# The handwritten orders of work of four engines, renewed from self-attention to the first products of the shared network

## The chip, the core and the metric

The kernel runs on one core of a Trainium2 chip. The metric is the device time of one launch in microseconds (us); lower is better. Engines are named as in the profile: PE multiplies matrices, PEld loads its weights, DVE (VectorE), ACT (ScalarE) and POOL (GpSimd) work on elements, SP issues most DMAs.

## What is computed

One decoder layer in fp32 for 8 batches of 112 tokens with 512 features (896 tokens): self-attention with latent queries and keys, cross-attention to a context, and a shared network with 16 routed experts, with a layer norm after each.

```python
x = layernorm(x + attn(x))      # 16 heads; q = [q_nope, rope(q_pe)], k = [k_nope, rope(k_rope)]; causal softmax
x = layernorm(x + xattn(x, ctx))  # 16 heads of 32; keys and values from ctx @ Wkv_expand.T; causal softmax
x = layernorm(x + shared(x) + routed(x))  # two shared gelu networks, top 2 of 16 experts
```

## The kernel before

Every product is split in three: `x = hi + lo`, and hi*hi, hi*lo and lo*hi are summed in PSUM. So a product's result is copied out of PSUM twice, by ACT (the hi part) and then by DVE (the lo part), before its bank is free.

**Self-attention** goes over 4 groups of 4 heads (`NG`, `GH`). Its steps are items of lists, one list for each engine, each item a kind and a number. Kinds: `A` (joined weights), `E` and `O` (rope products), `Q` (queries), `G` (scores, masked by DVE into `sT`), `S` (PE turns the scores, DVE takes the row maximum, ACT the four exponentials), `N` (DVE inverts the row sums, POOL multiplies them in), `T` (PE turns the probabilities, ACT and DVE split them), `B` (output weights joined with values), `Z` (probabilities times latents, split by ACT and DVE), `W` (the product of the group's output, added to `acc` by DVE), `SA` and `SB` (splitting weights that a DMA brought to `stage`), `R` (splitting the turned queries; SP then packs them with 16 DMAs for each half, line 557). `NEXT` marks an item of the following group. `turns` writes out a `..._PRE` list, the body in a loop of three passes (`ATT_PE` and so on), and a `..._LAST` list.

**Cross-attention** goes over 4 groups in the same way with `X_PRE`, `X_..` (three passes) and `X_LAST`. `K`, `Q`, `V` are keys, queries and values; `K` goes from DVE to SP, which spreads it with four DMAs (line 589) to `kb`, and PE waits for these before `S`. `Z` is copied by ACT and DVE to `zf`, and POOL splits it (lines 650 and 653) for `W`. `L`, `LK`, `X` split weights. In the last lists `STAT`, `VAR`, `ROOT`, `ROW` are steps of the layer norm, `U1` and `U2` turn its result, `F` (POOL) splits the first weights of the shared network, `FF` are its first products; `K` and `CX` in `ATT_LAST` begin cross-attention.

What orders the engines: each works through its own list and waits on semaphores inside an item. Products of the kinds A, E, O, Q, G, B, W, K and V take PSUM banks 6 and 7 in turn by their place in PE's list, and each waits until the one two places before has left its bank (`bank_free`). `S` waits for the exponentials of the score tile two before it, `T` for POOL's product, `Z` for the split of `T`.

The change touches the lists, the tile `warm` and `function_ready`, which calls a function once so that ACT loads its table early. After `X_LAST` the kernel runs 8 stages of the shared network with the expert blocks between them; the change leaves them as they are.

## Time and profile before

| | us |
|---|---|
| median of 3 runs (838.66 to 839.76) | 839.01 |
| the profiled execution | 837.5 |
| its span | 835.7 |
| PE busy | 816.4 (98%) |
| DVE busy | 530.9 (64%) |
| ACT busy | 456.7 (55%) |
| POOL busy | 241.1 (29%) |

The profile is of one execution. PE's matmuls are pipelined: one begins before the one before it has ended, so PE's lost time is read from the distances of starts. The loop of self-attention runs from 68.5 to 274.2 us (three passes), its last list to 322.8, cross-attention's loop from 338.6 to 423.7 (three passes), its last list to 458.

### The profile page before, as it was taken

The page shows a single profiled execution, that of the slowest core. Times are in us where ns is not written, and L with a number is a line of the kernel's source. Part 1 is how long each engine was busy: PE and PEld are TensorE (multiplying, and loading weights), DVE is VectorE, ACT ScalarE, POOL GpSimd, SP SyncE. Part 2 cuts the span into 40 slices and gives each one's busy share as a digit, 9 for nine tenths or more (in the row PEclk, how much of TensorE's full clock was granted, in tenths as well). Part 3 has the DMA queues.
Part 4 walks back from the last instruction along what each step waited for, and adds up shares of the span by engine and source line. Part 5 has one row for each costly group of instructions (what it writes and reads, how often), then busy time and mean ns, then how long its engine had stood idle before and what let it go on. Part 6 is the DMA issues. An engine that isn't in the chain of part 4 may idle for free.

```text
span 835.7 us, 13323 instructions
## 1 busy us (share of the span) xinstructions
PE 816.4 (98%) x4270; PEld 698.3 (84%) x4270; DVE 530.9 (64%) x994; ACT 456.7 (55%) x1189; POOL 241.1 (29%) x284
## 2 busy tenths in 40 slices
PE   7999999999999999999999999999999999999997
PEld 5887888888888888888867788888889888888885
DVE  4657746854854777778797566355655656656466
ACT  6427445643743666887786524254746737557050
POOL 0142311231132141655562005312332332320520
PEclk9999999999999999999999999999999999999999
DMA  9113413241260343312220306444555645634522
GB/s 347 66 45 114 179 56 85 92 168 41 72 230 17 83 163 93 88 41 58 56 74 1 101 3 226 150 125 140 190 181 173 227 140 176 211 131 139 141 73 89
DMA packets 42749, 99.99 MB, mean 120 GB/s; under 512 B 16016, under 2 KB 24080, under 8 KB 41584
## 3 DMA queue, kind: packets, MB, share of 16 engines
q1 hardware_dynamic: 31648, 61.62, 23.1%
q0 software_dynamic: 11056, 37.79, 13.9%
q8 instruction: 27, 0.44, 0.2%
q14 instruction: 18, 0.15, 0.1%
HBM read 71.59 MB, written 20.97 MB: 111 GB/s over the span
## 4 chain that ended last, share of the span: by engine, by line
PE 89%; DVE 4%; ACT 3%; issue 1%; DMA 1%; SPq 1%; DVEq 0%; ACTq 0%
PE ps L1553 71%; PE ps L1716 4%; PE ps L1900 2%; PE ps L1574 2%; PE ps L1613 2%; PE ps L1890 2%; PE ps L1724 1%; PE ps L1784 1%; ACT Pt L890 1%; DMA kb<-kx 1%; PE ps L1902 1%; SPq L589 1%; DVE stats L1173 1%; PE ps L1568 1%; PE ps L1605 0%
## 5 line engine op out<-in xcount | busy, mean ns | idle before, releaser
L645 POOL TENSOR_TENSOR Pt<-Pt,rowinv 112x448 f32<-112x448 f32 x64 | 59.6, 936 | 169.2 <-DVE rowinv L1157 169.0
L890 ACT ACTIVATE Pt<-ps,negmax 112x112 f32<-112x112 f32 x256 | 87.2, 358 | 26.9 <-DVE negmax L1150 26.4
L1553 PE MATMUL ps<-x2T_hi,ws_hi 128*128 128x448 f32 x256 | 95.3, 372 | 1.6 <-DVE x2T_lo L1094 1.6
L1553 PE MATMUL ps<-x2T_hi,ws_lo 128*128 128x448 f32 x256 | 93.6, 366 | 0.0
L1553 PE MATMUL ps<-x2T_lo,ws_hi 128*128 128x448 f32 x256 | 93.6, 365 | 0.0
L1553 PE MATMUL ps<-w_hi,h_hi 128*128 128x512 f32 x224 | 89.9, 401 | 0.0
L1021 ACT ACTIVATE hf<-ps,b 128x448 f32<-128x448 f32 x64 | 40.6, 634 | 88.0 <-PE ps L1553 87.3
L1553 PE MATMUL ps<-w_hi,h_lo 128*128 128x512 f32 x224 | 88.5, 395 | 0.0
L1553 PE MATMUL ps<-w_lo,h_hi 128*128 128x512 f32 x224 | 88.4, 395 | 0.0
L1094 DVE TENSOR_TENSOR h_lo<-hf,h_hi 128x448 fp32r<-128x448 f32 x64 | 39.9, 623 | 45.8 <-ACT h_hi L1022 45.6
L1439 DVE TENSOR_TENSOR acc<-ps,acc 128x512 f32<-128x512 f32 x56 | 38.6, 689 | 45.0 <-PE ps L1553 45.0
L769 POOL DMA_INDIRECT wg<-in_wtab,ix_i x29 | 31.0, 1069 | 112.0 <-DVE ix_i L1424 61.2
L1553 PE MATMUL ps<-qkT_hi,wa_hi 128*128 128x448 f32 x144 | 54.2, 377 | 1.3 <-DVE wa_lo L1097 0.6
L819 ACT ACTIVATE PT_hi<-ps 112x448 fp32r<-112x448 f32 x64 | 34.8, 545 | 37.2 <-PE ps L1613 37.1
L1167 DVE TENSOR_TENSOR acc<-ps,acc 128x512 f32<-128x512 f32 x56 | 38.6, 689 | 25.8 <-PE ps L1553 25.7
L890 ACT ACTIVATION_READ_ACCUMULATOR Pt<-ps,negmax 112x1 f32 x256 | 53.7, 210 | 0.0
L1553 PEld LDWEIGHTS ps<-x2T_hi,ws_hi 128*128 128x128 f32 x256 | 48.1, 188 | 6.4 <-POOL ws_lo L653 2.0
L1553 PE MATMUL ps<-qkT_hi,wa_lo 128*128 128x448 f32 x144 | 52.6, 366 | 0.0
L1553 PE MATMUL ps<-qkT_lo,wa_hi 128*128 128x448 f32 x144 | 52.6, 365 | 0.0
L1553 PEld LDWEIGHTS ps<-x2T_lo,ws_hi 128*128 128x128 f32 x256 | 48.2, 188 | 4.3
L1553 PEld LDWEIGHTS ps<-x2T_hi,ws_lo 128*128 128x128 f32 x256 | 48.1, 188 | 4.1
L1553 PEld LDWEIGHTS ps<-w_hi,h_lo 128*128 128x128 f32 x224 | 42.1, 188 | 10.1
(289 smaller groups left out, 2212.3 us busy)
## 6 DMA issues: line engine op xcount, KB each, us to landing
stage<-in_wf SPq DMA_DIRECT2D x30, 513.0 KB, 4.2
rows_in<-in_zeros SPq DMA_DIRECT2D x30, 256.0 KB, 5.5
xs<-rows_in POOLq DMA_DIRECT2D x29, 256.0 KB, 4.3
rows_out<-yb POOLq DMA_DIRECT2D x29, 256.0 KB, 2.7
stage<-in_wb SPq DMA_DIRECT2D x4, 1280.0 KB, 5.7
stage<-in_wa SPq DMA_DIRECT2D x8, 512.0 KB, 4.4
qr<-ro_hi SPq DMA_DIRECT2D x64, 56.0 KB, 1.9
qr<-ro_lo SPq DMA_DIRECT2D x64, 56.0 KB, 1.9
```

What stands on the lines that cost most here:

```text
L645: nc.gpsimd.tensor_tensor(p, p, rowinv[0:S, b % 2, :].unsqueeze(2).broadcast_to([S, GH, S]), ALU.mult).then_inc(norm_done, 1)
L769: return pool.indirect_dma_start(dst, None, table, bass.IndirectOffsetOnAxis(ap=index, axis=0))
L819: return nc.scalar.activation(dst, src, ACT.Copy, **kw)
L890: last = nc.scalar.activation(Pt[0:S, b % 2, h * S:(h + 1) * S], ps[0:S, b % 2, h * S:(h + 1) * S], ACT.Exp, bias=negmax[0:S, b % 2, h:h + 1],
L1021: nc.scalar.activation(hf[:, q % 4, :], ps[:, q % 3, 0:HALF], ACT.Gelu, bias=bias)
L1094: return nc.vector.tensor_tensor(dst, src, f32(hi), ALU.subtract)
L1167: nc.vector.tensor_tensor(acc[:, t, :], ps[:, 6 + at.bank, :], acc[:, t, :], ALU.add)\
L1439: V.tensor_tensor(acc2[:, t, :], ps[:, 3 + m % 2, :], (acc2 if n else acc)[:, t, :], ALU.add)\
L1553: ins = mm(dst, w, x, start=start and i == 0, stop=stop and i == len(ops) - 1, skip_group_check=not (start and stop))
L1574: ins = mm(ps[0:S, b, :], w, x, start=k == 0 and i == 0, stop=k == KD - 1 and i == 2, skip_group_check=True)
L1613: ins = nc.tensor.transpose(ps[0:S, 2 + b % 2, h * S:(h + 1) * S], Pt[0:S, b % 2, h * S:(h + 1) * S], ident[0:S, 0:S])
L1716: ins = mm(heads(bank[0:S, 0:GH * S]), w, x, start=i == 0, stop=i == len(ops) - 1)
```

## The change

The lists of PE, ACT, DVE and POOL are written in another order from the body of self-attention's loop to the last list of cross-attention; their items are the same (`SB`, `SA` and `R` do nothing on PE). `ATT_PRE` is unchanged. `warm` gets a second column, so that the call for Sqrt and the one for Exp write different elements. The core of the diff, with the lists of which the prediction speaks:

```diff
 ATT_PE = [
-    ("SB", 1), ("S", 0), ("G", 1), ("Q", 2, 1), ("G", 2), ("S", 1), ("B", 0), ("SB", 2), ("B", 1), ("T", 0), ("S", 2),
-    ("Q", 3, 1), ("B", 2), ("Z", 0), ("T", 1), ("G", 3), ("G", 4), ("Z", 1), (NEXT, "SA", 0), ("S", 3), ("S", 4),
-    ("T", 2), ("G", 5), (NEXT, "O", 0), ("B", 3), ("Z", 2), (NEXT, "SA", 1), ("S", 5), (NEXT, "E", 0), ("T", 3),
-    ("G", 6), ("W", 0), (NEXT, "A", 0), ("G", 7), (NEXT, "SA", 2), ("T", 4), (NEXT, "R", 0), ("Z", 3), ("W", 1),
-    (NEXT, "E", 1), (NEXT, "A", 1), ("S", 6), ("T", 5), ("Z", 4), ("S", 7), ("W", 2), (NEXT, "A", 2), ("Z", 5),
-    (NEXT, "O", 1), (NEXT, "R", 1), ("W", 3), ("T", 6), (NEXT, "Q", 0, 0), (NEXT, "Q", 1, 0), ("T", 7),
-    (NEXT, "Q", 2, 0), ("Z", 6), (NEXT, "SB", 0), ("W", 4), (NEXT, "Q", 3, 0), ("Z", 7), (NEXT, "Q", 0, 1), ("W", 5),
-    (NEXT, "G", 0), (NEXT, "Q", 1, 1), ("W", 6)]
+    ("S", 0), ("G", 1), ("Q", 2, 1), ("G", 2), ("S", 1), ("B", 0), ("B", 1), ("SB", 1), ("S", 2), ("T", 0),
+    (NEXT, "SA", 0), ("Q", 3, 1), ("B", 2), ("Z", 0), ("T", 1), ("G", 3), ("G", 4), ("B", 3), ("Z", 1), ("S", 3),
+    ("T", 2), ("S", 4), ("G", 5), (NEXT, "O", 0), ("G", 6), (NEXT, "SA", 1), ("T", 3), ("Z", 2), (NEXT, "E", 0),
+    ("S", 5), ("W", 0), ("G", 7), ("SB", 2), (NEXT, "R", 0), ("S", 6), ("Z", 3), (NEXT, "A", 0), ("T", 4), ("S", 7),
+    (NEXT, "E", 1), ("W", 1), (NEXT, "R", 1), (NEXT, "A", 1), (NEXT, "SB", 0), ("Z", 4), ("T", 5), ("W", 2),
+    (NEXT, "A", 2), (NEXT, "O", 1), ("W", 3), (NEXT, "Q", 0, 0), ("Z", 5), (NEXT, "Q", 1, 0), ("T", 6),
+    (NEXT, "Q", 2, 0), (NEXT, "Q", 3, 0), ("W", 4), ("T", 7), ("Z", 6), (NEXT, "G", 0), ("Z", 7), (NEXT, "Q", 0, 1),
+    ("W", 5), (NEXT, "SA", 2), (NEXT, "Q", 1, 1), ("W", 6)]
...
 ATT_ACT = [
     ("SB", 1), ("S", 0), ("Q", 2, 1), ("SB", 2), ("B", 0), ("B", 1), ("T", 0), ("S", 1), ("Q", 3, 1), ("B", 2),
-    ("Z", 0), ("T", 1), ("S", 2), (NEXT, "SA", 0), (NEXT, "SA", 1), ("T", 2), ("S", 3), ("Z", 1), ("B", 3), ("Z", 2),
-    ("T", 3), (NEXT, "SA", 2), (NEXT, "E", 0), ("S", 4), (NEXT, "A", 0), ("T", 4), ("Z", 3), (NEXT, "O", 0), ("S", 5),
-    (NEXT, "R", 0), ("T", 5), (NEXT, "A", 1), ("S", 6), ("Z", 4), (NEXT, "E", 1), (NEXT, "A", 2), ("Z", 5),
-    (NEXT, "O", 1), ("S", 7), (NEXT, "SB", 0), (NEXT, "Q", 0, 0), ("T", 6), (NEXT, "Q", 1, 0), (NEXT, "Q", 2, 0),
-    ("Z", 6), ("T", 7), (NEXT, "Q", 3, 0), (NEXT, "R", 1), ("Z", 7), (NEXT, "Q", 0, 1), (NEXT, "Q", 1, 1)]
+    ("T", 1), ("S", 2), (NEXT, "SA", 0), ("B", 3), ("Z", 0), ("T", 2), ("Z", 1), ("S", 3), (NEXT, "SA", 1),
+    (NEXT, "SA", 2), ("T", 3), ("Z", 2), ("S", 4), ("S", 5), (NEXT, "R", 0), (NEXT, "A", 0), ("Z", 3), ("T", 4),
+    (NEXT, "O", 0), (NEXT, "A", 1), ("Z", 4), (NEXT, "O", 1), ("T", 5), ("S", 6), (NEXT, "E", 0), (NEXT, "A", 2),
+    (NEXT, "Q", 0, 0), (NEXT, "E", 1), ("S", 7), ("Z", 5), (NEXT, "Q", 1, 0), ("T", 6), (NEXT, "Q", 2, 0),
+    (NEXT, "Q", 3, 0), (NEXT, "SB", 0), ("T", 7), ("Z", 6), ("Z", 7), (NEXT, "R", 1), (NEXT, "Q", 0, 1),
+    (NEXT, "Q", 1, 1)]
...
 ATT_DVE = [
-    ("S", 0), ("SB", 1), ("G", 1), ("N", 0), ("Q", 2, 1), ("G", 2), ("SB", 2), ("B", 0), ("S", 1), ("B", 1), ("T", 0),
-    ("N", 1), ("S", 2), ("Q", 3, 1), ("B", 2), ("T", 1), ("Z", 0), ("G", 3), ("N", 2), ("G", 4), ("S", 3),
-    (NEXT, "SA", 0), ("G", 5), ("T", 2), ("N", 3), ("Z", 1), (NEXT, "O", 0), ("S", 4), ("B", 3), (NEXT, "SA", 1),
-    (NEXT, "E", 0), ("G", 6), ("S", 5), (NEXT, "SA", 2), ("T", 3), ("W", 0), ("N", 4), ("Z", 2), (NEXT, "A", 0),
-    ("Z", 3), ("G", 7), ("T", 4), ("N", 5), ("W", 1), (NEXT, "E", 1), (NEXT, "A", 1), (NEXT, "R", 0), ("S", 6),
-    ("T", 5), ("N", 6), ("W", 2), ("Z", 4), (NEXT, "A", 2), (NEXT, "O", 1), ("S", 7), ("W", 3), ("N", 7),
-    (NEXT, "Q", 0, 0), ("Z", 5), ("T", 6), (NEXT, "Q", 1, 0), (NEXT, "Q", 2, 0), ("W", 4), ("T", 7), ("Z", 6),
-    (NEXT, "Q", 3, 0), (NEXT, "R", 1), (NEXT, "Q", 0, 1), (NEXT, "SB", 0), ("W", 5), ("Z", 7), (NEXT, "G", 0),
-    (NEXT, "Q", 1, 1), ("W", 6)]
+    ("S", 0), ("G", 1), ("SB", 1), ("N", 0), ("Q", 2, 1), ("G", 2), ("SB", 2), ("B", 0), ("S", 1), ("B", 1), ("T", 0),
+    ("N", 1), ("Q", 3, 1), ("B", 2), ("S", 2), ("G", 3), ("T", 1), ("N", 2), ("G", 4), (NEXT, "SA", 0), ("S", 3),
+    ("B", 3), ("S", 4), ("Z", 0), ("G", 5), ("N", 3), ("Z", 1), ("T", 2), (NEXT, "O", 0), (NEXT, "SA", 1), ("G", 6),
+    (NEXT, "E", 0), ("T", 3), ("S", 5), ("N", 4), ("Z", 2), (NEXT, "SA", 2), ("W", 0), (NEXT, "R", 0), ("N", 5),
+    ("G", 7), (NEXT, "A", 0), ("Z", 3), (NEXT, "E", 1), ("T", 4), ("W", 1), (NEXT, "A", 1), ("S", 6), ("T", 5),
+    ("W", 2), ("Z", 4), ("N", 6), ("S", 7), (NEXT, "A", 2), (NEXT, "O", 1), ("W", 3), (NEXT, "Q", 0, 0), ("N", 7),
+    (NEXT, "Q", 1, 0), ("Z", 5), ("T", 6), (NEXT, "Q", 2, 0), (NEXT, "Q", 3, 0), ("T", 7), ("W", 4), (NEXT, "SB", 0),
+    ("Z", 6), (NEXT, "G", 0), (NEXT, "Q", 0, 1), ("Z", 7), (NEXT, "R", 1), ("W", 5), (NEXT, "Q", 1, 1), ("W", 6)]
...
 ATT_LAST_PE = [
-    ("SB", 1), ("SB", 2), ("S", 0), ("G", 1), ("Q", 2, 1), ("G", 2), ("T", 0), ("B", 0), ("B", 1), ("S", 1),
-    ("Q", 3, 1), ("B", 2), ("S", 2), ("Z", 0), ("T", 1), ("G", 3), ("B", 3), ("Z", 1), ("S", 3), ("G", 4), ("T", 2),
-    ("W", 0), ("Z", 2), ("S", 4), ("G", 5), ("T", 3), ("G", 6), ("S", 5), ("W", 1), ("T", 4), ("Z", 3), ("S", 6),
-    ("G", 7), ("Z", 4), ("W", 2), ("S", 7), ("T", 5), ("W", 3), ("T", 6), ("Z", 5), ("K", 0), ("Z", 6), ("T", 7),
+    ("SB", 1), ("S", 0), ("G", 1), ("Q", 2, 1), ("G", 2), ("S", 1), ("B", 0), ("B", 1), ("S", 2), ("T", 0),
+    ("Q", 3, 1), ("B", 2), ("Z", 0), ("T", 1), ("G", 3), ("G", 4), ("B", 3), ("S", 3), ("Z", 1), ("S", 4), ("G", 5),
+    ("T", 2), ("W", 0), ("Z", 2), ("G", 6), ("T", 3), ("S", 5), ("W", 1), ("T", 4), ("Z", 3), ("S", 6), ("G", 7),
+    ("Z", 4), ("W", 2), ("SB", 2), ("S", 7), ("T", 5), ("W", 3), ("T", 6), ("Z", 5), ("T", 7), ("K", 0), ("Z", 6),
     ("W", 4), ("W", 5), ("Z", 7), ("U1", 0), ("U1", 1), ("U1", 2), ("U1", 3), ("W", 6)]
...
 ATT_LAST_ACT = [
-    ("SB", 1), ("S", 0), ("Q", 2, 1), ("SB", 2), ("B", 0), ("T", 0), ("B", 1), ("S", 1), ("Q", 3, 1), ("B", 2),
...
+    ("SB", 1), ("S", 0), ("Q", 2, 1), ("SB", 2), ("B", 0), ("B", 1), ("T", 0), ("S", 1), ("Q", 3, 1), ("B", 2),
...
 ATT_LAST_DVE = [
-    ("S", 0), ("SB", 1), ("G", 1), ("N", 0), ("Q", 2, 1), ("G", 2), ("SB", 2), ("B", 0), ("S", 1), ("T", 0), ("B", 1),
-    ("N", 1), ("Q", 3, 1), ("B", 2), ("S", 2), ("Z", 0), ("T", 1), ("G", 3), ("N", 2), ("B", 3), ("Z", 1), ("S", 3),
...
-    ("W", 3), ("N", 7), ("T", 6), ("VAR1", 0), ("Z", 5), ("ROOT1", 0), ("Z", 6), ("K", 0), ("ROW1", 2), ("W", 4),
-    ("ROW1", 3), ("T", 7), ("W", 5), ("VAR1", 1), ("Z", 7), ("U1", 0), ("U1", 1), ("ROOT1", 1), ("U1", 2), ("U1", 3),
...
+    ("S", 0), ("SB", 1), ("G", 1), ("N", 0), ("Q", 2, 1), ("G", 2), ("SB", 2), ("B", 0), ("S", 1), ("B", 1), ("T", 0),
+    ("S", 2), ("N", 1), ("Q", 3, 1), ("B", 2), ("T", 1), ("G", 3), ("G", 4), ("Z", 0), ("N", 2), ("S", 3), ("B", 3),
...
+    ("N", 7), ("W", 3), ("T", 6), ("Z", 5), ("VAR1", 0), ("Z", 6), ("K", 0), ("ROOT1", 0), ("ROW1", 2), ("T", 7),
+    ("W", 4), ("ROW1", 3), ("W", 5), ("Z", 7), ("VAR1", 1), ("U1", 0), ("U1", 1), ("ROOT1", 1), ("U1", 2), ("U1", 3),
...
 X_PE = [
-    ("Z", 1), ("S", 5), ("T", 3), ("S", 6), ("Z", 2), (NEXT, "K", 0), ("Z", 3), ("T", 4), (NEXT, "Q", 0), ("T", 5),
-    (NEXT, "V", 0), ("S", 7), (NEXT, "S", 0), (NEXT, "K", 1), ("Z", 4), ("W", 0), ("T", 6), ("Z", 5), ("T", 7),
-    ("W", 1), (NEXT, "S", 1), ("W", 2), (NEXT, "Q", 1), ("Z", 6), (NEXT, "S", 2), (NEXT, "T", 0), (NEXT, "S", 3),
-    ("W", 3), ("Z", 7), (NEXT, "V", 1), (NEXT, "T", 1), ("W", 4), (NEXT, "S", 4), (NEXT, "Z", 0), (NEXT, "T", 2),
-    ("W", 5), ("W", 6)]
+    ("Z", 1), ("S", 5), ("T", 3), ("S", 6), ("Z", 2), (NEXT, "K", 0), ("T", 4), ("Z", 3), (NEXT, "Q", 0), ("S", 7),
+    ("T", 5), (NEXT, "K", 1), (NEXT, "V", 0), (NEXT, "S", 0), ("Z", 4), ("T", 6), ("Z", 5), (NEXT, "S", 1), ("W", 0),
+    ("T", 7), (NEXT, "Q", 1), ("W", 1), ("Z", 6), (NEXT, "T", 0), ("Z", 7), (NEXT, "S", 2), ("W", 2), (NEXT, "T", 1),
+    (NEXT, "S", 3), ("W", 3), (NEXT, "V", 1), (NEXT, "S", 4), ("W", 4), (NEXT, "Z", 0), (NEXT, "T", 2), ("W", 5),
+    ("W", 6)]
...
 X_ACT = [
-    ("S", 4), ("Z", 1), ("T", 3), (NEXT, "L"), ("S", 5), (NEXT, "K", 0), ("X",), ("T", 4), ("S", 6), ("Z", 3),
-    (NEXT, "Q", 0), ("T", 5), (NEXT, "V", 0), ("S", 7), (NEXT, "K", 1), ("T", 6), (NEXT, "S", 0), ("Z", 5), ("T", 7),
-    (NEXT, "S", 1), (NEXT, "Q", 1), (NEXT, "T", 0), (NEXT, "S", 2), ("Z", 7), (NEXT, "V", 1), (NEXT, "T", 1),
+    ("S", 4), ("Z", 1), (NEXT, "L"), ("T", 3), ("X",), (NEXT, "K", 0), ("T", 4), ("S", 5), (NEXT, "Q", 0), ("S", 6),
+    ("Z", 3), (NEXT, "K", 1), ("T", 5), ("S", 7), (NEXT, "V", 0), ("Z", 5), ("T", 6), (NEXT, "S", 0), ("T", 7),
+    (NEXT, "S", 1), (NEXT, "Q", 1), (NEXT, "T", 0), ("Z", 7), (NEXT, "T", 1), (NEXT, "S", 2), (NEXT, "V", 1),
     (NEXT, "S", 3), (NEXT, "T", 2)]
...
 X_DVE = [
-    ("Z", 1), ("N", 4), ("T", 2), ("S", 5), ("T", 3), (NEXT, "K", 0), ("N", 5), ("S", 6), ("T", 4), ("N", 6),
-    ("Z", 3), (NEXT, "Q", 0), ("S", 7), (NEXT, "V", 0), ("T", 5), ("N", 7), (NEXT, "K", 1), ("W", 0), ("T", 6),
-    (NEXT, "S", 0), ("W", 1), (NEXT, "S", 1), (NEXT, "N", 0), ("Z", 5), (NEXT, "N", 1), (NEXT, "Q", 1), ("W", 2),
-    ("T", 7), (NEXT, "T", 0), (NEXT, "S", 2), ("W", 3), ("Z", 7), (NEXT, "N", 2), (NEXT, "S", 3), ("W", 4),
-    (NEXT, "V", 1), (NEXT, "T", 1), (NEXT, "N", 3), (NEXT, "S", 4), ("W", 5), ("W", 6)]
+    ("Z", 1), ("T", 2), ("N", 4), ("S", 5), ("T", 3), (NEXT, "K", 0), ("N", 5), ("S", 6), (NEXT, "Q", 0), ("T", 4),
+    ("N", 6), ("S", 7), ("Z", 3), ("T", 5), ("N", 7), (NEXT, "K", 1), (NEXT, "V", 0), (NEXT, "S", 0), ("Z", 5),
+    ("T", 6), (NEXT, "S", 1), (NEXT, "N", 0), ("W", 0), (NEXT, "N", 1), ("T", 7), (NEXT, "Q", 1), (NEXT, "S", 2),
+    ("W", 1), ("W", 2), ("Z", 7), (NEXT, "S", 3), ("W", 3), (NEXT, "T", 0), (NEXT, "N", 2), (NEXT, "T", 1),
+    (NEXT, "S", 4), (NEXT, "V", 1), ("W", 4), (NEXT, "N", 3), ("W", 5), ("W", 6)]
...
 X_LAST_DVE = [
-    ("Z", 1), ("T", 2), ("N", 4), ("S", 5), ("T", 3), ("S", 6), ("N", 5), ("Z", 3), ("T", 4), ("S", 7), ("W", 0),
-    ("N", 6), ("T", 5), ("Z", 4), ("N", 7), ("W", 1), ("STAT2", 0), ("Z", 5), ("W", 2), ("T", 6), ("W", 3),
-    ("STAT2", 1), ("STAT2", 2), ("STAT2", 3), ("VAR2", 0), ("T", 7), ("ROOT2", 0), ("ROW2", 2), ("ROW2", 3), ("Z", 6),
-    ("W", 4), ("Z", 7), ("STAT2", 4), ("U2", 0), ("U2", 1), ("W", 5), ("U2", 2), ("U2", 3), ("W", 6), ("STAT2", 5),
-    ("STAT2", 6), ("VAR2", 1), ("ROOT2", 1), ("FF", 0), ("U2", 4), ("ROW2", 6), ("U2", 5), ("U2", 6), ("FF", 1),
+    ("N", 4), ("T", 2), ("Z", 1), ("S", 5), ("T", 3), ("S", 6), ("N", 5), ("Z", 3), ("T", 4), ("W", 0), ("S", 7),
+    ("Z", 4), ("N", 6), ("T", 5), ("STAT2", 0), ("W", 1), ("W", 2), ("N", 7), ("STAT2", 1), ("Z", 5), ("W", 3),
+    ("STAT2", 2), ("STAT2", 3), ("T", 6), ("VAR2", 0), ("T", 7), ("ROOT2", 0), ("Z", 6), ("ROW2", 2), ("W", 4),
+    ("Z", 7), ("ROW2", 3), ("U2", 0), ("U2", 1), ("U2", 2), ("U2", 3), ("W", 5), ("STAT2", 4), ("W", 6), ("STAT2", 5),
+    ("STAT2", 6), ("VAR2", 1), ("ROOT2", 1), ("ROW2", 6), ("U2", 4), ("U2", 5), ("U2", 6), ("FF", 0), ("FF", 1),
     ("FF", 2), ("FF", 3)]
...
 X_LAST_POOL = [
-    ("Z", 1), ("N", 4), ("X",), ("N", 5), ("Z", 3), ("N", 6), ("N", 7), ("Z", 4), ("F", 2), ("Z", 5), ("Z", 6),
-    ("Z", 7), ("F", 3)]
+    ("N", 4), ("X",), ("Z", 1), ("N", 5), ("Z", 3), ("N", 6), ("Z", 4), ("N", 7), ("Z", 5), ("Z", 6), ("Z", 7),
+    ("F", 2), ("F", 3)]
...
-        warm = sb("warm", [P, 1])
+        warm = sb("warm", [P, 2])
...
-            nc.scalar.activation(warm[:, :], one[:, :], ACT.Sqrt)
+            nc.scalar.activation(warm[:, 0:1], one[:, :], ACT.Sqrt)
...
-                nc.scalar.activation(warm[:, :], one[:, :], func)
+                at = 0 if func == ACT.Sqrt else 1
+                nc.scalar.activation(warm[:, at:at + 1], one[:, :], func)
```

## Rows read from the trace of the kernel before

**Rows 1.** The page: busy us of each engine, share of the span, instructions.
```profile
PE 816.4 (98%) x4270; PEld 698.3 (84%) x4270; DVE 530.9 (64%) x994; ACT 456.7 (55%) x1189; POOL 241.1 (29%) x284
```

**Rows 2.** Windows: stretch, length; busy PE, PEld, DVE, ACT, POOL; PE clock; DMA share, GB/s.
```profile
205.57:274.14 68.57, 68.56 (x370) 59.23 (x369) 43.40 (x76) 34.44 (x103) 16.14 (x14) 1.00 0.32 106
395.36:423.74 28.38, 28.21 (x164) 24.45 (x163) 21.67 (x46) 21.68 (x90) 16.02 (x21) 1.00 0.19 42
434.00:438.00 4.00, 2.45 (x13) 1.42 (x11) 3.92 (x9) 2.47 (x4) 3.77 (x8) 1.00 0.64 236
438.00:442.00 4.00, 3.73 (x11) 2.42 (x12) 3.85 (x13) 2.35 (x6) 0.51 (x3) 0.57 0.00 0
```

**Rows 3.** Timeline (start, us, what), first pass of self-attention, DVE and PE.
```profile
69.98 1.22 DVE L1094 TENSOR_TENSOR ws_lo<-stage,ws_hi 128x1024 fp32r<-128x1024 f32 x1 [1.22 <-ACT ws_hi L819]
71.02 0.37 PE L1553 MATMUL ps<-qkT_lo,wa_hi 128*128 128x448 f32 x1
71.22 0.37 PE L1553 MATMUL ps<-qkT_hi,wa_lo 128*128 128x448 f32 x1
71.79 0.46 PE L1716 MATMUL ps<-qa_hi,qkT_hi 128*112 128x448 f32 x1 [0.20 <-DVE sT L1259]
```

**Rows 4.** Timeline, third pass of self-attention, POOL and PE at the third tile.
```profile
219.01 0.93 POOL L645 TENSOR_TENSOR Pt<-Pt,rowinv 112x448 f32<-112x448 f32 x1 [3.11 <-DVE rowinv L1157]
219.03 1.12 PE L1724 MATMUL ps<-ident,sT 112*112 112x112 f32 x8
220.00 0.59 PE L1613 MATMUL ps<-ident,Pt 112*112 112x112 f32 x4
```

**Rows 5.** Timeline, last group of self-attention, PE and DVE.
```profile
281.17 0.47 PE L1553 MATMUL ps<-qkT_hi,wa_hi 128*128 128x448 f32 x1 [0.34 <-DVE ws_lo L1094]
...
309.24 0.70 DVE L1173 BATCH_NORM_STATS2 stats<-acc 128x6 f32<-128x512 f32 x1
...
310.58 0.47 PE L1553 MATMUL ps<-PT_hi,kvN_hi 112*128 112x448 f32 x1 [0.49 <-DVE PT_lo L1094]
```

**Rows 6.** Timeline of SP in self-attention: packing of a half of the queries.
```profile
267.17 4.95 SPq L557 DMA_DIRECT2D qr<-ro_hi  x8
```

**Rows 7.** Timeline and chain, second pass of cross-attention: keys to their scores.
```profile
370.82 0.36 PE L1553 MATMUL ps<-cx_hi,wx_lo 128*128 128x448 f32 x1
371.46 0.56 ACT L819 ACTIVATE kx<-ps 128x448 fp32r<-128x448 f32 x1
374.65 2.49 DMA kb<-kx
377.19 0.40 PE L1605 MATMUL ps<-identb,maskb 112*112 112x448 bf16 x1 [0.20 <-DMA kb<-kx]
```

**Rows 8.** Timeline, last group of cross-attention, PE, POOL and DVE.
```profile
427.50 0.45 PE L1553 MATMUL ps<-PT_hi,vN_hi 112*128 112x448 f32 x1 [0.28 <-DVE PT_lo L1094]
434.81 1.04 POOL L650 TENSOR_TENSOR ws_hi<-w1f,one 128x512 fp32r<-128x512 f32 x1
438.11 0.60 PE L1553 MATMUL ps<-wx_hi,zx_hi 128*128 128x512 f32 x1 [0.83 <-issue]
438.51 0.63 PE L1553 MATMUL ps<-wx_lo,zx_hi 128*128 128x512 f32 x1
442.62 0.69 DVE L1173 BATCH_NORM_STATS2 stats<-acc 128x6 f32<-128x512 f32 x1
444.55 0.68 DVE L1167 TENSOR_TENSOR acc<-ps,acc 128x512 f32<-128x512 f32 x1
446.57 0.45 PE L1553 MATMUL ps<-x2T_hi,ws_hi 128*128 128x448 f32 x1 [1.61 <-DVE x2T_lo L1094]
```

**Rows 9.** Timeline, first products of the shared network, ACT and PE.
```profile
450.88 1.28 ACT L1021 ACT_TABLE_LOAD   x1
452.71 0.63 ACT L1022 ACTIVATE h_hi<-ps,b 128x448 fp32r<-128x448 f32 x1
455.52 0.45 PE L1553 MATMUL ps<-x2T_hi,ws_hi 128*128 128x448 f32 x1
```

More of the change, by code:

```diff
@@ L164 @@
 ATT_POOL = [
-    ("N", 0), ("N", 1), ("N", 2), ("N", 3), ("N", 4), (NEXT, "O", 0), (NEXT, "R", 0), ("N", 5), ("N", 6), ("N", 7),
-    (NEXT, "O", 1), (NEXT, "R", 1)]
+    ("N", 0), ("N", 1), ("N", 2), ("N", 3), ("N", 4), (NEXT, "O", 0), ("N", 5), (NEXT, "R", 0), (NEXT, "O", 1),
+    ("N", 6), ("N", 7), (NEXT, "R", 1)]
 ATT_LAST_PE = [
[4 rows of a table removed]
[4 rows of a table added]
     ("W", 4), ("W", 5), ("Z", 7), ("U1", 0), ("U1", 1), ("U1", 2), ("U1", 3), ("W", 6)]
 ATT_LAST_ACT = [
[5 rows of a table removed]
-ATT_LAST_DVE = [
[6 rows of a table removed]
[5 rows of a table added]
+ATT_LAST_DVE = [
[6 rows of a table added]
     ("W", 6), ("VAR1", 2), ("ROOT1", 2), ("ROW1", 6)]
@@ L189 @@
 ATT_LAST_POOL = [
-    ("N", 0), ("N", 1), ("N", 2), ("N", 3), ("N", 4), ("LK",), ("KZ",), ("N", 5), ("N", 6), ("CX",), ("N", 7), ("L",)]
+    ("N", 0), ("N", 1), ("N", 2), ("LK",), ("N", 3), ("N", 4), ("N", 5), ("KZ",), ("N", 6), ("CX",), ("N", 7), ("L",)]
 X_DONE = [("K", 0)]
 X_PRE_PE = [
-    ("U1", 4), ("U1", 5), ("Q", 0), ("V", 0), ("U1", 6), ("S", 0), ("S", 1), ("K", 1), ("V", 1), ("S", 2), ("T", 0),
+    ("U1", 4), ("U1", 5), ("Q", 0), ("U1", 6), ("V", 0), ("S", 0), ("S", 1), ("K", 1), ("V", 1), ("S", 2), ("T", 0),
@@ L196 @@
     ("Q", 1), ("S", 3), ("T", 1), ("Z", 0), ("S", 4), ("T", 2)]
 X_PRE_ACT = [
-    ("U1", 4), ("U1", 5), ("Q", 0), ("EXP",), ("V", 0), ("U1", 6), ("S", 0), ("K", 1), ("V", 1), ("S", 1), ("T", 0),
-    ("S", 2), ("Q", 1), ("T", 1), ("S", 3), ("T", 2)]
+    ("U1", 4), ("U1", 5), ("Q", 0), ("EXP",), ("U1", 6), ("V", 0), ("S", 0), ("K", 1), ("S", 1), ("T", 0), ("S", 2),
+    ("Q", 1), ("V", 1), ("T", 1), ("S", 3), ("T", 2)]
 X_PRE_DVE = [
-    ("Q", 0), ("U1", 4), ("U1", 5), ("S", 0), ("V", 0), ("U1", 6), ("N", 0), ("S", 1), ("K", 1), ("S", 2), ("N", 1),
@@ L202 @@
-    ("V", 1), ("T", 0), ("N", 2), ("Q", 1), ("S", 3), ("T", 1), ("S", 4), ("N", 3)]
+    ("U1", 4), ("Q", 0), ("U1", 5), ("S", 0), ("V", 0), ("U1", 6), ("N", 0), ("S", 1), ("K", 1), ("S", 2), ("N", 1),
+    ("T", 0), ("N", 2), ("Q", 1), ("S", 3), ("T", 1), ("S", 4), ("N", 3), ("V", 1)]
 X_PRE_POOL = [("F", 0), ("N", 0), ("N", 1), ("N", 2), ("F", 1), ("N", 3)]
 X_PE = [
-    ("Z", 1), ("S", 5), ("T", 3), ("S", 6), ("Z", 2), (NEXT, "K", 0), ("Z", 3), ("T", 4), (NEXT, "Q", 0), ("T", 5),
-    (NEXT, "V", 0), ("S", 7), (NEXT, "S", 0), (NEXT, "K", 1), ("Z", 4), ("W", 0), ("T", 6), ("Z", 5), ("T", 7),
@@ L223 @@
+    ("W", 1), ("W", 2), ("Z", 7), (NEXT, "S", 3), ("W", 3), (NEXT, "T", 0), (NEXT, "N", 2), (NEXT, "T", 1),
+    (NEXT, "S", 4), (NEXT, "V", 1), ("W", 4), (NEXT, "N", 3), ("W", 5), ("W", 6)]
 X_POOL = [
-    (NEXT, "LK"), ("N", 4), (NEXT, "L"), ("Z", 1), ("N", 5), ("Z", 3), ("X",), ("N", 6), ("N", 7), ("Z", 5),
-    (NEXT, "N", 0), (NEXT, "N", 1), (NEXT, "N", 2), ("Z", 7), (NEXT, "N", 3)]
+    (NEXT, "LK"), ("N", 4), (NEXT, "L"), ("Z", 1), ("N", 5), ("X",), ("N", 6), ("Z", 3), ("N", 7), ("Z", 5),
@@ L228 @@
+    (NEXT, "N", 0), (NEXT, "N", 1), ("Z", 7), (NEXT, "N", 2), (NEXT, "N", 3)]
 X_LAST_PE = [
[2 rows of a table removed]
[2 rows of a table added]
     ("U2", 2), ("U2", 3), ("W", 5), ("W", 6), ("FF", 0), ("FF", 1), ("U2", 4), ("FF", 2), ("U2", 5), ("U2", 6),
```

22 rows, old and new, of tables (ATT_LAST_ACT, ATT_LAST_DVE, X_LAST_ACT, X_LAST_PE) are left out of this document.

## The prediction

> **What bounds the kernel now.** I read the page first, then the windows by pass, then PE's timeline in the whole stretch that the lists order (68 to 458 us), looking at the distances between starts, and last what DVE, ACT, POOL and SP did ahead of each hole. PE is busy for 98% of the span [rows 1]. A pass of self-attention takes 68.57 us, and PE is busy for 68.56 of them; a pass of cross-attention takes 28.38 us with 28.21 busy [rows 2]. DVE and ACT are at 43 and 34 of 68 us, and at 21.7 of 28.4. The matmuls are the same before and after, so a new order can only give back holes. The reader should see how little there is: the order can't take from a pass what PE computes in it.
>
> A hole is larger by starts than by its bracket: in the first pass two matmuls in a row start 0.20 us apart, and at the wait for `sT` it is 0.57, with a bracket of 0.20 [rows 3]. So I take each bracket plus 0.17. The holes are: one before `G2` in the first pass [rows 3]; a short one in each pass at the third tile [rows 4]; two in the last group [rows 5]; one in each pass of cross-attention, at a DMA [rows 7]; and a bundle in the last group of cross-attention, where from 434 to 438 us PE is busy for 2.45 of 4 us while DVE is busy for 3.92 [rows 2]. There, and only there, DVE is the bound.
>
> **The change part by part.**
>
> First pass. DVE's list has `SB1` ahead of `G1`, and ACT's `SB1` comes late because of a table load, so `SB1` starts on DVE only at 69.98, takes 1.22, and `G1`, whose bank `G2` needs, comes after it [rows 3]. The change puts `G1` first. Gain 0.57 - 0.20 = 0.37. What is late next is the `B0` product, which needs `SB1` split: in the list it stands `Q2`, `G2` and `S1` later, which is more than the 1.22 us. Ends 0 and 0.5; I take 0.4.
>
> Third tile of each pass. PE turns `S3` and `S4` together from 219.03 and goes on to `T2` at 220.00, just after POOL's product, which ends at 219.01 + 0.93 = 219.94 [rows 4]. The change puts `B3` before these and `S4` behind `T2`. But on DVE it moves `S2`'s row maximum behind `Q3` and `B2`, and the exponentials, POOL's product and `T2` follow from that. ACT had `T1` ahead of `S2` in effect anyway, so I count that delay as 0.1 to 0.4 us, while PE now has `B3` more and `S4` less ahead of `T2`, some 0.3 us. Gain a pass between -0.3 and 0.2; I take 0.1, so 0.3 for three passes, with ends -0.9 and 0.6.
>
> Other moves within the passes. I laid each engine's new list beside PE's, with PE gapless, and asked of each item what it waits for. Bank turnarounds (ACT's copy and DVE's subtraction) have covers of 0.1 to 0.6 us at `Q3`, `A0`, `O1`, `W3`, `W4`, `W5`; none is negative. `R` of the second half moves on ACT behind `Z6` and `Z7`, some 1.6 us later. With it go 16 DMAs on SP: 8 take 4.95 us to issue [rows 6], so 9.9 us together, and what waits is `G4` of the next pass. Before, the issue ends near 267.2 + 9.9 = 277.1, and `G4` runs near 286 (274.2, the start of the group, and 11.6 us of PE's items), so 1.6 us are hidden with about 5 to spare after the landing. Were the cover gone, each us would cost one a pass. `W`, `G` and the zero rows queued on SP keep their order. I cost these at nothing, and put the risk in the rivals.
>
> Last group of self-attention. ACT has `T0` ahead of `B1`, with `S1` alone between `B1` and `Q3` on PE; the wait before `Q3` is 0.34 [rows 5], 0.5 by starts. With the order of the loop, where only a rest of 0.15 stays by the same reading, the gain is 0.35. The second hole is 0.49 [rows 5], 0.65 by starts: `Z6` waits for `T6`'s split, which DVE does behind `W3` and its statistics (309.24 to 309.94). The change puts `T7` into the hole on PE; `T6` stays behind `W3`, so some 0.25 stays. Gain 0.4. DVE then has less time for `W4`, `W5` and `Z7` ahead of `W6`: 0 to 0.4 lost, I take 0.1. Sum 0.65, ends 0 and 1.
>
> Cross-attention, three passes. `K0`'s last matmul starts at 370.82, but ACT copies it only at 371.46, after the exponentials of `S5`; DVE, four DMA issues and a landing (2.49) follow, and `S0` starts at 377.19 after a bracket of 0.20 [rows 7]. The change puts `K0` ahead of `S5` on ACT, and `K1` (three matmuls, 0.6 us) ahead of `S0` on PE. Both push in one direction: the copy can start 0.3 us earlier and the cover grows by 0.6. The hole of 0.20 + 0.17 closes: 1.1 for three passes. Late next is `S5`'s softmax with `T5`; PE has `Q0` and `S7` ahead of it, 3.2 us by count. Ends 0 and 1.3.
>
> Last group of cross-attention. The first product of the shared network (446.57) waits 1.61 us for DVE's split of `U2` number 3 [rows 8]. Before that, DVE does the addition of `W5` (444.55, 0.68) and the statistics of tile 4 (442.62, 0.69) [rows 8]. The change puts both behind it: 0.60 + 0.70 by starts = 1.3. Also, `Z3` waited 0.28 at 427.50 [rows 8]; `T4` now stands before it, and `X`, `STAT` and `N` are spread otherwise, so DVE's unbroken run begins up to 0.6 earlier. On POOL `F2` (from 434.81, two parts of 1.0 to 1.1 us) moves out of the way of `Z5`, whose product `W4` waited 0.83 for at 438.11 [rows 8]; this counts only through DVE. Against it, `N7` moves behind `W1` and `W2`: `T7` starts about 1.2 us later, but its split had waited for DVE's statistics for 3 us, which is the cover. Gain 1.9, ends 0 and 2.4.
>
> Behind it. Gelu's table load takes 1.28 at 450.88, the first gelu ends at 453.34, and `FF3`, which needs it, starts at 455.52 [rows 9]: a cover of 2.2. The change puts `U2` 4 ahead of `FF0` on ACT and starts `FF0` on PE earlier, which by my count leaves 0.1 to 0.5. Cost 0, end 0.5. The Trainium skill's page ScalarE: Activation LUTs (section Rules for kernel authors) asks for about 2.7 us for each switch to another set of tables. By that figure `FF3` would wait some 1.3 us and the gain of this stretch would be a third of what I take; the row with 1.28 decides for me.
>
> `warm` as two columns costs nothing: the same calls with the same table loads.
>
> Sum: 0.4 + 0.3 + 0.65 + 1.1 + 1.9 = 4.35, say 4.4 us. Against the profiled execution, 837.5 (span 835.7 and 1.8 around it), this gives 833.1. The median of the runs is 839.0, 1.5 above that execution, so the forecast is 834.6. From the first product of the shared network on PE is the bound, so what is won ahead of it stays.
>
> **The rivals.** (a) The clock. From 438 to 442 us the granted clock is 0.57, so mostly at the lower of its two levels, 1.2 GHz, after a stretch in which PE was busy for 2.45 of 4 us [rows 2]. There a 512-column matmul starts 0.40 us after the one before it [rows 8]. Today this falls on work that waits for DVE anyway. The new order has PE wait longer ahead of `U2`. If the low level reaches `FF0`, its 12 matmuls at 0.37 instead of 0.20 cost 2.0 us: 836.6. The Trainium skill's page TensorE: Matmul & The Clock Gate (What's actually happening) says that it is idleness that halves the clock, which speaks for this rival. Against it: the clock was back well ahead of 446.57, through a wait of 1.61.
>
> (b) Given back. In the tail the late `N7` becomes the bound in DVE's place: `T7`, `Z7` and the copies of `U2` shift by its 1.2 us, the 1.28 us of the table load for Sqrt follow, and 1.9 shrinks to nothing. And the banks with 0.1 to 0.3 us of cover turn into waits, 0.3 us in each of six passes, 1.8 of the other 2.5. What is left is 0.7, so 838.3. For it: eight such covers by my count. Against it: DVE is idle for a third of a self-attention pass.
>
> (c) Slower. In cross-attention DVE now does `T0`, `N2`, `T1`, `S4`, `V1`, `W4`, `N3` in a row at the end of a pass, about 3.4 us by starts, while PE runs `V1`, `S4`, `W4`, `Z0`, `T2`, `W5`, `W6` in 4.4 us. `W5` needs `V1`'s bank, `W6` needs `W4`'s. I count covers of 0.2 and 0.3 us. If DVE enters this row late, PE waits for it in full, in each of three passes. It decides from 2.1 us a pass (6.3, against a gain of 4.4): then the time is 841 or more. Against it, DVE is idle for 6.7 of 28.4 us in a pass, so it rarely enters late.
>
> (d) It does nothing: the waits are set by semaphores elsewhere and PE's holes only move. 839.0, part of (b).
>
> **How the numbers follow.** Forecast 834.6 with 0.67, its own range 832.3 to 836.4. (a) 0.10 at 836.6. (b) with (d) 0.15 at 837.5 to 839.5. (c) 0.08 at 841. The measurement can tell 0.2% (1.7 us) from no change, so faster means under 837.3: 0.67 + 0.10 + 0.01 of (b) = 0.78. Same is 0.14 and slower 0.08. The range runs from 832.2 (all terms at their good ends, 0.5 + 0.6 + 1.0 + 1.3 + 2.4 = 5.8, and 1 more for holes under 0.12) to 838.5, which takes in (a) and the near part of (b).
>
> **What would show it.** Right: no bracket at `S0` with kb<-kx as its releaser; no wait at `G2` in the first pass; one short wait left in the last group; the first product of the shared network starts 4 to 5 us earlier than at 446.57, of which about 2 after the loop's end; the rest to the end of the same length. Wrong: a pass of self-attention over 68.6 or of cross-attention over 28.4; a granted clock below 1 in the window of `FF0`; a wait before `FF3`; brackets of `W5` or `W6` on DVE.

## The result and the profile after

The changed kernel takes 851.02 us (846.91 to 852.98), against 839.12 beside it: 1.4% slower, a ratio of 1.0142 (1.0123 to 1.016). The forecast was 834.6, with a range from 832.2 to 838.5. The profiled execution took 852.83 us, with a span of 851.0.

The page of the changed kernel, busy time by engine, and the granted clock in 40 slices:

```profile
PE 826.7 (97%) x4270; PEld 706.4 (83%) x4270; DVE 536.2 (63%) x994; ACT 457.6 (54%) x1189; POOL 241.5 (28%) x284
...
PEclk9999899999989999999999999999999999999999
```

The instructions are as many as in [rows 1], and yet PE is busy for 10.3 us more and DVE for 5.3 us more. A busy time that grows at the same count means that single instructions became longer. Two slices at 8 of the granted clock lie in the loop of self-attention.

Distances of starts on PE, in us, by stretch (one profiled execution of each of five kernels; the last three are experiments below):

| from, to | before | after | SA2' moved | and V1', W4 | and tail filled |
|---|---|---|---|---|---|
| start, first product `B0` | 73.22 | 74.28 | 73.31 | 73.60 | 73.78 |
| three passes of self-attention | 205.57 | 220.94 | 205.55 | 205.32 | 205.36 |
| last group, to `U1` | 39.11 | 38.40 | 38.40 | 38.36 | 38.38 |
| `U1` to the last `W6` of cross-attention's loop | 105.15 | 105.43 | 105.39 | 104.01 | 103.96 |
| last group, to the shared network | 23.52 | 22.97 | 22.19 | 23.55 | 22.16 |
| the rest | 389.1 | 389.0 | 389.0 | 389.0 | 389.0 |

The whole loss, 15.4 us, is in three passes. (The 1.06 more of the first row lie ahead of the first item that the change moves, and they come and go between executions: with SA2' moved the same stretch takes 73.31.) The passes are 74.18, 72.65 and 74.11 us long. Windows of the changed kernel: a pass of self-attention and one of cross-attention (to set beside [rows 2]), then the stretch in the second pass in which the loss arises:

```profile
148.46:221.11 72.65, 70.38 (x370) 60.79 (x369) 46.07 (x77) 35.81 (x105) 16.08 (x14) 0.98 0.30 99
410.49:439.05 28.56, 28.35 (x165) 24.16 (x163) 20.93 (x45) 21.85 (x89) 16.11 (x21) 1.00 0.19 41
171.00:173.00 2.00, 0.51 (x3) 0.14 (x1) 2.00 (x2) 0.94 (x1) 0.94 (x1) 1.00 0.00 0
173.00:175.00 2.00, 1.25 (x10) 1.25 (x11) 1.22 (x4) 0.01 (x1) 1.21 (x2) 0.94 0.55 82
175.00:177.00 2.00, 2.00 (x13) 2.00 (x13) 0.66 (x2) 1.29 (x3) 1.76 (x1) 0.50 0.95 404
177.00:179.00 2.00, 2.00 (x9) 1.80 (x9) 0.56 (x2) 0.17 (x1) 0.00 (x0) 0.71 1.02 431
```

Two things follow on each other. From 171 to 173 PE does almost nothing, and DVE is busy in all of it with two instructions. From 175 on PE is busy all the time, until 177 at a granted clock of 0.50, the lower of its two levels (1.2 GHz). The timeline of the same stretch, POOL, DVE and PE:

```profile
168.80 0.93 POOL L645 TENSOR_TENSOR Pt<-Pt,rowinv 112x448 f32<-112x448 f32 x1 [5.90 <-DVE rowinv L1158]
169.69 1.15 POOL L683 TENSOR_TENSOR rt<-rt,ru 128x448 f32<-128x448 f32 x1
170.80 1.14 POOL L684 TENSOR_TENSOR rt<-rt,ru 128x448 f32<-128x448 f32 x1
...
169.15 3.87 DVE L1095 TENSOR_TENSOR wa_lo<-stage,wa_hi 128x1024 fp32r<-128x1024 f32 x1
172.95 0.68 DVE L1168 TENSOR_TENSOR acc<-ps,acc 128x512 f32<-128x512 f32 x1
...
171.15 0.37 PE L1554 MATMUL ps<-PT_hi,kvN_lo 112*128 112x448 f32 x1
173.75 0.32 PE L1554 MATMUL ps<-wa_hi 128*128 128x128 f32 x1 [2.24 <-DVE acc L1168]
```

`SA2'` (the third piece of the next group's weights, split by DVE) takes 3.87 us. The same instruction takes 1.21 or 1.22 where POOL is idle. It starts while POOL multiplies for `N4`, and it ends at 173.02, which is 1.08 behind the end of POOL's second addition for `O0'` (170.80 + 1.14 = 171.94). Behind it stands the addition of `W0`, whose bank `A0'` on PE needs; `A0'` also needs the split itself. PE is 2.40 us late by starts, in each of the three passes. In the kernel before, POOL did the same two additions from 233.17 on in the third pass, some 2.5 us after the end of `SA2'` (229.49, 1.22).

The changed kernel has a second, smaller case of this, and the kernel before shows what is not held. First `SA0'` in the second pass of the changed kernel, which takes 0.95 in the kernel before; then, from the third pass of the kernel before, a DVE instruction that reads one of its sources from PSUM:

```profile
157.32 0.93 POOL L645 TENSOR_TENSOR Pt<-Pt,rowinv 112x448 f32<-112x448 f32 x1 [3.29 <-DVE rowinv L1158]
157.80 1.27 DVE L1095 TENSOR_TENSOR wa_lo<-stage,wa_hi 128x768 fp32r<-128x768 f32 x1
```

```profile
233.17 1.15 POOL L683 TENSOR_TENSOR rt<-rt,ru 128x448 f32<-128x448 f32 x1
...
233.34 0.69 DVE L1097 SCALAR_TENSOR_TENSOR wa_lo<-ps,wa_hi 128x512 fp32r<-128x512 f32 x1 [0.63 <-ACT wa_hi L819]
```

`SA0'` ends 0.82 behind POOL's product, and nobody waits for it. The instruction of 233.34 lies inside POOL's and takes 0.69, as it does where POOL is idle (242.55 in the same pass).

What became of the predicted holes, and the new ones. PE in the changed kernel:

```profile
72.55 0.36 PE L1554 MATMUL ps<-qkT_hi,wa_lo 128*128 128x448 f32 x1
72.75 0.37 PE L1717 MATMUL ps<-qa_hi,qkT_hi 128*112 128x448 f32 x1
...
326.31 0.37 PE L1554 MATMUL ps<-cx_hi,wx_lo 128*128 128x448 f32 x1
326.69 0.47 PE L1554 MATMUL ps<-PT_hi,kvN_hi 112*128 112x448 f32 x1
...
381.15 0.47 PE L1554 MATMUL ps<-wx_hi,zx_hi 128*128 128x512 f32 x1 [0.21 <-DVE vN_lo L1095]
...
452.94 0.47 PE L1554 MATMUL ps<-wx_hi,zx_hi 128*128 128x512 f32 x1 [0.63 <-DVE acc L1168]
454.51 0.58 PE L1554 MATMUL ps<-PT_hi,vN_hi 112*128 112x448 f32 x1 [0.64 <-DVE PT_lo L1095]
462.02 0.45 PE L1554 MATMUL ps<-x2T_hi,ws_hi 128*128 128x448 f32 x1 [0.69 <-DVE x2T_lo L1095]
```

`G2` follows at 0.20 where [rows 3] had 0.57. In the last group of self-attention the holes of [rows 5] are smaller, by starts 0.49 instead of 0.88 at `Q3` and 0.38 instead of 0.85 at `Z6`. In cross-attention the wait for the keys [rows 7] is gone, but each pass has a new one ahead of `W5`, for DVE's `V1'`. The shared network waits 0.69 where [rows 8] had 1.61.

### The profile page after: what moved, and what is told of

Same layout as the page of the kernel before. It is cut to its first block, busy times and chain, and to the rows that moved or that the text cites. A ratio compares the mean times of both kernels' runs of the same rounds, so it can differ in the third digit from the quotient of the medians.

```text
span 851.0 us, 13323 instructions
## 1 busy us (share of the span) xinstructions
PE 826.7 (97%) x4270; PEld 706.4 (83%) x4270; DVE 536.2 (63%) x994; ACT 457.6 (54%) x1189; POOL 241.5 (28%) x284
## 4 chain that ended last, share of the span: by engine, by line
PE 93%; DVE 3%; issue 2%; ACT 1%; DMA 0%; DVEq 0%
PE ps L1554 73%; PE ps L1717 4%; PE ps L1614 3%; PE ps L1575 2%; PE ps L1901 2%; PE ps L1785 2%; PE ps L1891 1%; PE ps L1725 1%; PE ps L1903 1%; PE ps L1606 1%; PE ps L1569 1%; PE ps L1641 1%; DVE acc L1168 0%; PE ps L1814 0%; DVE wa_lo L1095 0%
## 5 line engine op out<-in xcount | busy, mean ns | idle before, releaser
L1554 PE MATMUL ps<-qkT_hi,wa_hi 128*128 128x448 f32 x144 | 56.1, 390 | 1.0 <-DVE wa_lo L1098 0.6
L1554 PEld LDWEIGHTS ps<-w_lo,h_hi 128*128 128x128 f32 x224 | 42.2, 188 | 9.2
```

The lines of the kernel that those rows point to most:

```text
L1554: ins = mm(dst, w, x, start=start and i == 0, stop=stop and i == len(ops) - 1, skip_group_check=not (start and stop))
```

## The experiments

The theory was that DVE and POOL hold each other up, and that the half clock is a consequence of PE's hole. Rivals were DVE's order alone, and a clock that falls by itself. The diffs of lists show only the items around the one that is moved.

**SA2' earlier on DVE.** Nothing else is changed.

```diff
 ATT_DVE = [
-    ("G", 6), (NEXT, "E", 0), ("T", 3), ("S", 5), ("N", 4), ("Z", 2), (NEXT, "SA", 2), ("W", 0),
+    ("G", 6), (NEXT, "SA", 2), (NEXT, "E", 0), ("T", 3), ("S", 5), ("N", 4), ("Z", 2), ("W", 0),
```

> The changed kernel with one item of DVE's list moved: the subtraction of the third piece of A's weights (SA2') goes from behind Z2 to directly behind G6, three items ahead of where POOL's N4 and O0' run. Theory A (DVE and POOL hold each other up: the subtraction has two sources in SBUF and waits until POOL's three operations in a row are done): SA2' takes 1.21 us instead of 3.87, the addition of W0 starts some 2.7 us earlier, PE's 2.24 us wait for the bank of A0' goes in each of three passes, and with it the half clock behind it; a pass takes 68.4 to 68.8 us instead of 72.6 to 74.2, the whole 835 to 838. Theory B (only DVE's order, that is W0 queued too far back, no mutual hold-up): the same items stand between, so the wait stays above 1.5 us and the whole above 848. Theory C (the clock falls by itself, not because of the wait): the wait goes but windows at half clock stay behind it, the whole is 842 to 846.

Measured: 836.03 us, ratio 0.9965 (0.9953 to 0.9976). Timeline of DVE and PE, second pass:

```profile
158.97 1.21 DVE L1096 TENSOR_TENSOR wa_lo<-stage,wa_hi 128x1024 fp32r<-128x1024 f32 x1
...
164.53 0.36 PE L1555 MATMUL ps<-PT_hi,kvN_lo 112*128 112x448 f32 x1
164.74 0.22 PE L1555 MATMUL ps<-wa_hi 128*128 128x128 f32 x1
```

Its windows, the whole pass and the 6 us behind `A0'`:

```profile
141.86:210.37 68.51, 68.49 (x370) 59.38 (x369) 43.56 (x77) 35.66 (x105) 16.12 (x14) 1.00 0.31 105
165.00:171.00 6.00, 6.00 (x39) 5.42 (x39) 2.91 (x5) 2.30 (x4) 3.62 (x3) 1.00 1.04 418
```

One item of one list is worth 15 us. DVE's 77 instructions of the pass take 43.56 us instead of 46.07, `A0'` follows at 0.21, and the clock stays at 1. What is left is a kernel faster than before: the rest of the change does gain.

**W0 ahead of SA2'.**

```diff
 ATT_DVE = [
-    ("Z", 2), (NEXT, "SA", 2), ("W", 0), (NEXT, "R", 0),
+    ("Z", 2), ("W", 0), (NEXT, "SA", 2), (NEXT, "R", 0),
```

> The changed kernel with DVE's W0 put ahead of SA2' instead of behind it; POOL runs as before beside SA2'. Theory A: SA2' starts 0.6 us later and still ends 1.1 us after POOL's last addition (some 3.2 us long), near 173.0 of the second pass; A0' needs all three pieces of A, so PE's hole shrinks by only about 0.7 us and the half clock may stay; the whole 845 to 850. Theory B (the queue in front of W0 is all): the hole goes, the whole is 835 to 839.

Measured: 846.31 us. Timeline, second pass:

```profile
169.91 1.14 POOL L685 TENSOR_TENSOR rt<-rt,ru 128x448 f32<-128x448 f32 x1
...
169.24 2.90 DVE L1096 TENSOR_TENSOR wa_lo<-stage,wa_hi 128x1024 fp32r<-128x1024 f32 x1
...
172.19 0.33 PE L1555 MATMUL ps<-wa_hi 128*128 128x128 f32 x1 [1.56 <-DVE wa_lo L1096]
```

The split ends at 172.14, again 1.09 behind POOL (171.05). The wait names the split itself now, as the theory had it; putting `W0` first does not help. The passes are 73.48, 70.27 and 70.24 us: two lost only the hole, one the clock too. The two splits start during different POOL operations, the product and the first addition, and end the same 1.1 us behind POOL's last one.

**PE computes through the hole.**

```diff
                 kind, j = item[0], item[-1] if len(item) < 3 else item[1]
+                if item == ("A", 0) and not isinstance(g, int):
+                    pe.wait_ge(pt_free, B * g - B + 5)
+                    for i in range(12):
+                        mm(ps[0:S, 2, 0:4 * S], kvN_hi[0:S, 0, 0:S], PT_hi[0:S, 0, :],
+                           start=True, stop=True, skip_group_check=True)
```

> The changed kernel with 12 matmuls of 448 columns, whose result nobody reads, put on PE ahead of A0' of each pass (about 2.4 us, into a bank that is free), so that PE computes through the hole and its length stays. Theory A says that the half clock is a consequence of the hole: the granted clock stays at 1 in the 8 us behind it, a pass takes 71.0 to 71.4 us instead of 72.6 to 74.2, the whole is 842 to 845. Theory C (the clock falls by itself, or by what the other engines do): windows at half clock stay, the filler changes nothing, 849 to 853.

Measured: 844.04 us, with passes of 71.03, 71.04 and 70.96. PE around the hole of the second pass, then windows of the third:

```profile
167.12 0.36 PE L1554 MATMUL ps<-PT_hi,kvN_lo 112*128 112x448 f32 x1
167.32 2.56 PE L1655 MATMUL ps<-PT_hi,kvN_hi 112*112 112x448 f32 x12
169.73 0.32 PE L1554 MATMUL ps<-wa_hi 128*128 128x128 f32 x1
```

```profile
215.48:286.44 70.96, 70.94 (x381) 61.29 (x381) 45.91 (x77) 34.41 (x104) 16.08 (x14) 1.00 0.31 102
```

The split is as long as before (3.88) and `A0'` as late, but the clock is 1. So the loss falls in two, in the profiled executions: 213.03 - 205.57 = 7.5 us for the hole itself, and 220.94 - 213.03 = 7.9 us for the half clock behind it (7.0 by the medians, 851.02 - 844.04). 36 matmuls whose result nobody reads made the kernel 7 us faster. The Trainium skill's page TensorE: Matmul & The Clock Gate (What's actually happening) has idleness as the cause of the low clock, and this run agrees.

**The collision put into the kernel before.** First POOL's item alone, then DVE's too:

```diff
 ATT_POOL = [
-    ("N", 0), ("N", 1), ("N", 2), ("N", 3), ("N", 4), (NEXT, "O", 0), (NEXT, "R", 0), ("N", 5),
+    ("N", 0), ("N", 1), ("N", 2), ("N", 3), (NEXT, "O", 0), ("N", 4), (NEXT, "R", 0), ("N", 5),
```

> The kernel before with one item of POOL's list moved: O0' goes ahead of N4, so that its two additions run as soon as the two products are there, at about 228.3 of the third pass instead of 233.17, beside DVE's SA2' (229.49, 1.22 us). DVE's list is that of before. Theory A: SA2' takes 2.0 to 2.5 us instead of 1.22, since it ends about 1.1 us after POOL's second addition; W0 is 0.9 to 1.2 us late and PE waits 0.3 to 1 us for A0' in each pass; the whole is 840 to 842.5. Theory B (durations are fixed, only the order of each list counts): SA2' stays at 1.22, the whole at 838.5 to 839.5.

```diff
 ATT_DVE = [
-    ("G", 6), ("S", 5), (NEXT, "SA", 2), ("T", 3), ("W", 0),
+    ("G", 6), ("S", 5), ("T", 3), (NEXT, "SA", 2), ("W", 0),
```

> The kernel before with O0' ahead of N4 on POOL, as in the run with that edit alone, and SA2' on DVE one item later, behind T3. Then SA2' starts at about 230.03 of the third pass, 0.55 later, while POOL's second addition (from 229.47) is under way. Theory (of two operations that need the same way into SBUF, the one that comes second is held until the other is done): SA2' takes 1.6 to 1.75 us instead of 1.22 and ends 1.08 behind POOL's addition, and that addition is back at 1.15 us from 2.24. Rival (POOL always gives way to DVE in this kernel's order): SA2' stays at 1.22 and POOL's addition is again over 2 us. The time of the whole is within 1 us of the kernel before by both.

Measured: 838.76 us with the first edit (ratio 0.9995, 0.9986 to 1.0005), one execution of 840.12 with both. The first, POOL and DVE in the third pass:

```profile
229.47 2.24 POOL L684 TENSOR_TENSOR rt<-rt,ru 128x448 f32<-128x448 f32 x1
...
229.49 1.22 DVE L1094 TENSOR_TENSOR wa_lo<-stage,wa_hi 128x1024 fp32r<-128x1024 f32 x1
```

With both edits:

```profile
231.12 1.15 POOL L684 TENSOR_TENSOR rt<-rt,ru 128x448 f32<-128x448 f32 x1
...
231.68 1.67 DVE L1094 TENSOR_TENSOR wa_lo<-stage,wa_hi 128x1024 fp32r<-128x1024 f32 x1
...
233.41 0.33 PE L1553 MATMUL ps<-wa_hi 128*128 128x128 f32 x1 [0.36 <-DVE wa_lo L1094]
```

In the first run I had expected DVE to be held, and that was wrong: DVE and POOL came at almost the same time, DVE kept its 1.22, and POOL's addition was drawn out from 1.15 to 2.24, to 1.00 behind DVE's end. Nobody waits for it at once, so the time stays. In the second, DVE comes 0.56 later, and the roles change: 1.15 on POOL, 1.67 on DVE (expected 1.6 to 1.75), ending 1.08 behind POOL's end. The passes become 69.19 us, 0.6 more. So it is a mutual hold, in the kernel before too. With 0.56 between the starts, the one that comes second pays; with 0.02 between them the starts don't say which that is. I had expected a time within 1 us of the kernel before; the one execution lies 1.0 above its median of 839.11, and the passes show a loss that I hadn't counted.

**O0' ahead of N4 on POOL, in the changed kernel.** The same edit of `ATT_POOL` as above.

> The changed kernel with one item of POOL's list moved: O0' ahead of N4. DVE's list is untouched, SA2' starts at about 169.15 of the second pass as before, in the middle of O0's two additions; N4's product follows without a gap and ends near 170.7. Theory A1 (DVE gets in only when POOL has no further operation ready): SA2' takes 2.5 to 2.8 us, PE's hole at A0' shrinks from 2.24 to about 1.1, the whole 842 to 847. Theory A2 (DVE gets in at the end of the one POOL operation that runs when it comes): SA2' takes 1.6 to 2.0 us and POOL's N4 is drawn out instead, the hole is under 0.6, the whole 836 to 841. Rival B (no mutual hold-up, order on DVE only): SA2' stays at 3.87 and the whole at 849 to 853.

Measured: 837.44 us, ratio 0.9986 (0.9975 to 0.9998). Third pass:

```profile
231.30 1.16 POOL L684 TENSOR_TENSOR rt<-rt,ru 128x448 f32<-128x448 f32 x1
232.40 2.83 POOL L645 TENSOR_TENSOR Pt<-Pt,rowinv 112x448 f32<-112x448 f32 x2
...
231.68 1.85 DVE L1095 TENSOR_TENSOR wa_lo<-stage,wa_hi 128x1024 fp32r<-128x1024 f32 x1
...
234.27 0.32 PE L1554 MATMUL ps<-wa_hi 128*128 128x128 f32 x1 [0.23 <-DVE acc L1168]
```

DVE waits for one POOL operation instead of three: 1.85 = (231.30 + 1.16 - 231.68) + 1.07, and now POOL's next product is drawn out (2 in 2.83 us instead of 1.8). The bracket of `A0'` falls to 0.23, the clock does not fall, and a pass is 68.96. Theory A2 held here. Since only POOL's list differs from the changed kernel, this also shows that it is POOL that stretches the split. Yet in the changed kernel DVE was passed over twice more, so which engine is let in at the end of an operation isn't settled. Both times POOL went on to an addition of `O0'` (lines 683 and 684), and here it had `N4`'s product (line 645) next; whether that decides, no run tests.

**Cross-attention's lists alone.** All lists that begin with `X_` from the changed kernel, the others of before.

> The kernel before with only the lists of cross-attention taken from the changed kernel (all names that begin with X_); the lists of self-attention and their last group are those of before. Theory (the whole loss sits in the loop of self-attention): the cross-attention passes are 0.1 to 0.2 us longer each, the last group about 1.3 shorter, as in the traces of the changed kernel with SA2' moved; the whole 837.5 to 838.8. Rival (the slower case of the prediction: DVE's long row at the end of a cross-attention pass makes up part of the loss): over 841.

Measured: 838.07 us, ratio 0.9982 (0.9973 to 0.9992). Passes of 28.53 and 28.56, the last group 23.45. The loss isn't here. The passes are a little longer, as expected; the last group should have given 1.3 and gave nothing in this execution, with a granted clock of 0.85 in it.

**V1' and W4 earlier on DVE, and the tail.** Each with SA2' moved.

```diff
 X_DVE = [
-    ("W", 3), (NEXT, "T", 0), (NEXT, "N", 2), (NEXT, "T", 1), (NEXT, "S", 4), (NEXT, "V", 1), ("W", 4),
+    ("W", 3), (NEXT, "T", 0), (NEXT, "N", 2), (NEXT, "V", 1), (NEXT, "T", 1), (NEXT, "S", 4), ("W", 4),
```

> The changed kernel with SA2' behind G6 on DVE, as in the run with that edit alone (836.0), and in the loop of cross-attention DVE's V1' moved two items forward, ahead of T1' and S4'. Theory: PE's wait for the bank of V1' ahead of W5 (0.21, 0.45 by starts) goes, a pass takes 28.3 us instead of 28.55, the whole 0.5 to 0.9 less than with the first edit alone: 835.1 to 835.6. Rival: T1' or S4' become late in its place and the passes stay at 28.5: 836.

Measured: 835.74 us, ratio 0.9962 (0.9948 to 0.9977), passes of 28.53 and 28.55. The pass of 28.3 did not come, but not for the rival's reason: the wait had moved one product on. PE:

```profile
365.00 0.40 PE L1555 MATMUL ps<-wx_hi,zx_lo 128*128 128x512 f32 x1
365.50 0.47 PE L1555 MATMUL ps<-wx_hi,zx_hi 128*128 128x512 f32 x1
```

`W5` follows without a wait and `W6` starts 0.50 after the last matmul of `W5` instead of 0.23: it waits for the bank of `W4`. With `("W", 4)` also ahead of `(NEXT, "S", 4)`:

> The kernel with SA2' and V1' moved (835.7), and in the loop of cross-attention DVE's addition W4 also moved, ahead of S4'. With V1' forward alone, a pass stayed at 28.54 us, since a gap of 0.26 by starts opened ahead of W6, whose bank W4's addition frees. Theory: with W4's addition 0.6 us earlier that gap closes too, a pass takes 28.2 to 28.35 us, the whole 834.8 to 835.4. Rival: S4' becomes late in its place and a wait of the same size opens at its softmax; a pass stays at 28.5, the whole 835.7 to 836.

Measured: 835.30 us, ratio 0.9955 (0.9941 to 0.9969), passes of 28.06 and 28.10, more than expected. But the last group took 23.55 instead of 22.2. Before that, on the kernel of 835.74, four items of this group had been moved (`N7`, `Z5` and `T6` ahead of statistics on DVE, `Z6` ahead of the root on ACT):

> The kernel of the run before (SA2' and V1' moved) with four items of the last group of cross-attention moved: on DVE N7 ahead of the statistics of tile 0, Z5 ahead of those of tile 1, T6 ahead of those of tile 2; on ACT Z6 ahead of the root. Theory: DVE is the bound up to the variances, so these come at the same time, but T7 starts 0.7 us and Z6 1 us earlier, ACT is free for the rows 0.6 us earlier, and the first product of the shared network comes 0.5 to 1 us earlier; the whole 834.4 to 835.1. Rival: the root and the table load for it move behind Z6 on ACT and take the gain back: same as the run before, 835.1 to 835.6.

Measured: 836.00 us, ratio 0.997 (0.9959 to 0.9981). The theory failed, and the rival only in part held: there was no gain, but the time lies above its range too, and the cause was another. `T7` started without a wait, but its split on DVE stood behind the variances, which came no earlier; `Z7` waited 1.27 for it, and the clock fell there (0.57 from 438 to 442).

**The tail filled.** The kernel of 835.30, with unread matmuls on PE:

```diff
                 m = NG * B + B * g
+                fill = {("T", 7): 3, ("W", 4): 4, ("Z", 6): 4, ("U2", 0): 3}
+                if isinstance(g, int) and g == NG - 1 and item in fill:
+                    pe.wait_ge(exp_done, m + 9)
+                    for i in range(fill[item]):
+                        mm(ps[0:S, 0, 0:4 * S], cx_hi[:, 0, :],
+                           cx_hi[:, 0:4, :].rearrange("p b s -> p (b s)"),
+                           start=True, stop=True, skip_group_check=True)
```

> The kernel with SA2', V1' and W4 moved (835.3), and in the last group of cross-attention 14 matmuls of 448 columns whose result nobody reads, ahead of T7 (3), W4 (4), Z6 (4) and U2 number 0 (3) on PE, where its waits are 0.7 to 0.9 us by starts. In the run without them the passes of cross-attention gave 1.4 us, and the last group took 1.3 us more (23.55 from the last product of the loop to the first of the shared network, against 22.2), with the transpositions of U2 at half clock. Theory: the low clock follows from the four waits in a row; with PE computing through them the granted clock stays at 1 up to the shared network, the last group takes 22.1 to 22.5 us, and the whole is 833.8 to 834.6. Rival: the low clock there has another cause, or the added matmuls end late and cost what they save; the whole is 835.2 to 836.

Measured: 834.73 us, ratio 0.9954 (0.994 to 0.9968). The last group without and with them, windows of two kernels:

```profile
421.29:444.84 23.55, 21.03 (x94) 15.59 (x93) 21.04 (x51) 17.55 (x60) 13.75 (x21) 0.86 0.21 65
```

```profile
421.48:443.64 22.16, 21.15 (x108) 15.34 (x107) 20.84 (x51) 17.38 (x60) 13.42 (x21) 1.00 0.23 69
```

The mechanism held in the trace: clock 1, 1.4 us less in the profiled execution. In the times a gain isn't shown. The median is 0.6 lower and lies between the ranges of theory and rival; against the kernel before measured beside each, the two kernels stand 3.8 and 4.0 us lower, with intervals that overlap almost wholly. Nor had the clock fallen equally without the added matmuls: its mean was 0.995 to 0.999 in those five executions. The kernel has the lowest median of those run, 4.0 us under the kernel before (838.76) and 16 under the changed kernel.

## Why the prediction was wrong

**The step that failed** is "Other moves within the passes", costed at nothing. I had laid the new lists beside PE's with each duration as in the trace of before, and found a positive cover at `A0`. The list of DVE alone did hold it: with 1.21 us `SA2'` would end at 170.36 and `W0`'s addition near 171.0 by my estimate, and `A0'` was due at 171.35. What I did not ask is which operations of DVE and POOL come to lie side by side. In DVE's old list `N4`, which releases POOL's product, stands three items behind `SA2'`; in the new one it stands two items ahead. So POOL's product and its two additions move from behind `SA2'` onto it, and the durations themselves change: 3.87 us for 1.21. What the prediction put at nothing cost 15.4 us in three passes, 7.5 for the hole at `A0'` and 7.9 for the half clock behind it. Of its own signs of being wrong, a pass over 68.6 us and a bracket at `W5` came.

The trace of before had a small instance. Here the subtraction of `SB0'` takes 0.73 beside POOL's split of the turned queries (`R`), against 0.68 without it; DVE and POOL:

```profile
266.95 0.73 DVE L1094 TENSOR_TENSOR wa_lo<-stage,wa_hi 128x512 fp32r<-128x512 f32 x1
...
265.01 2.13 POOL L704 TENSOR_TENSOR ro_lo<-rt,ro_hi 128x896 fp32r<-128x896 f32 x1 [9.12 <-ACT ro_hi L819]
```

POOL ends at 267.14, DVE 0.54 later. I did not read this row. The rule was also to be had: the Trainium skill's page SBUF — State Buffer (Who interferes with whom) says that a DVE instruction with two SBUF inputs contends with a GpSimd (POOL) instruction that reads SBUF, and that the ports they share are an exclusive lock. The traces agree on the splits of `wa` (1.67, 1.85, 2.90 and 3.87 for 1.21), and on POOL's side (2.24 for 1.15). The same section of the Trainium skill has the order of issue decide who blocks; by the starts, POOL's two additions came after `SA2'` (169.69 and 170.80 against 169.15) and went ahead of it, so the order of starts doesn't account for the 3.87.

**The clock** was a rival (0.10), with 2.0 us in `FF0`. The kind was right and the place and size were wrong: 7.9 us, behind the hole in self-attention. I had no hole of that size in the loop, so no place for it.

**The slower rival** (0.08) named another mechanism, DVE's long row in cross-attention. Its sign was there, a bracket of 0.21 at `W5`, but at 0.45 us a pass by starts, not the 2.1 from which it would decide. The chance of slower was far too small: it was taken for one mechanism, where lists written anew for every engine have many places at which two engines meet afresh.

**The terms**, read with SA2' moved, where the collision doesn't cover them:
- First pass: predicted 0.4; the hole of `G2` (0.37) is gone, but `B0` now starts 0.20 late; what is left as gain is 0.26 (from the last matmul of the first score product to `B0` 8.72 us instead of 8.98).
- Passes of self-attention: predicted 0.3; 0.0. The gap at the third tile went, others of 0.17 to 0.19 came.
- Last group of self-attention: predicted 0.65; 0.71. Right.
- Cross-attention passes: predicted 1.1; -0.24. The wait for the keys went as described, and a wait of 0.45 by starts took its place. I had counted 0.2 and 0.3 of cover at `W5` and `W6`; the first was negative, and so was the second once the first was mended (0.26 by starts). With both mended the 1.1 came (105.15 to 104.01).
- Last group of cross-attention: predicted 1.9; 1.33 with the clock at 1 (0.93 in that stretch before), 0.55 in the changed kernel with 0.93. So part of the gain is clock, not order. Rival (b) had it right that `N7` behind `W1` and `W2` becomes late: `T7` waits 0.54 for POOL's product.
- Gelu: predicted 0; the rest has the same length, and `FF3` starts without a wait. Right. The table load takes 1.28 at 468.25 of the changed kernel and the activation follows at 469.55; the first gelu ends at 470.71, 0.14 ahead of `FF3`.
- The packing of [rows 6]: I took 4.95 for both halves, but the second (from 272.15) takes 5.92, so the issue ends at 278.1 and not at 277.1. Nothing hung on it: no wait shows at `G4`.

The sum of what came is 2.1 in place of 4.4, from two profiled executions. The medians say 3.1 (836.03 against 839.17); the other 1.0 I can't assign, since the profiled execution of before lies 1.5 under its median.

## What to carry to other kernels

Durations in a trace hold only beside the neighbours they were measured with. Before two lists are shifted against each other, look at each DVE instruction with both sources in SBUF, and at what POOL does then. A busy time that grows while the count of instructions stays is the sign of such a hold, and it shows as no idle time and no releaser. And a wait on PE costs more than its length where the granted clock falls behind it: test it by letting PE compute something useless through the wait.

## What was not expected of the hardware

- One instruction was held for 2.66 us, over three POOL operations in a row, though it had come during the first. In the run with `O0'` first it was let in after one. Why, these runs don't show.
- Behind holes of 2.24 us the clock halved in all three passes of the profiled execution, behind holes of 1.56 us in one of three. In the last group of cross-attention it fell among four waits of 0.7 to 0.9 us by starts in some executions, and stayed at 1 in others with nearly the same waits (23.55 and 22.19 us for the group). The half clock cost as much as the hole, 7.9 against 7.5 us, and accounts for much of the spread of 846.9 to 853.0: the mean clock of these runs was 0.994 to 0.985, and with PE computing through the hole the runs lie between 843.9 and 844.4.
